# Three-part gathers and block-diagonal node products in a four-layer graph network on one core

## The chip, the cores and the metric

The kernel runs on one core of one Trainium2 chip. The metric is the device time of one execution in microseconds (us). A kernel's time is the median of its runs; one more execution is taken by the hardware profiler, and all rows come from that one.

## What is computed

The input has 6250 nodes with 64 features (`x`) and 200000 edges with a source, a destination, weights and attributes; the edges are sorted by destination. Four layers each compute `x = layernorm(x + layer(x))`:

```python
# layer 0: two spline convolutions (messages from two node products, mean by destination)
# layer 1: aggregation with attention over sources and over destinations
cat = jnp.concatenate((out, opinion, inn, inn_opinion), axis=1)
return cat @ weight + bias
# layer 2: three GCN convolutions, widths 16, 32 and 64
h = x @ w;  out = segment_sum(norm[:, None] * h[row], col);  return out + b
x2 = relu(gcn_conv(x, w1, b1, ...)); x3 = relu(gcn_conv(x2, w2, b2, ...)); x4 = relu(gcn_conv(x3, w3, b3, ...))
return jnp.concatenate([x, x4], axis=1) @ lw + lb
# layer 3: attention with a softmax over each destination's edges
score = leaky_relu(s_src + s_dst + s_edge, 0.2)
alpha = exp(score - max_per[dst]) / (denom[dst] + 1e-08)
out = segment_sum((z[src] + e) * alpha[:, None], dst);  return out + x
```

## The kernel before, in words

**Nodes.** A node array is held as 128 partitions x 49 node rows (`J` = 49) x features, in SBUF. A node product (`dense`, L83) multiplies every row by a small float32 weight matrix, 7 node rows (`GROUP_SLOTS`) at a time, so in 7 groups. For each group ScalarE copies the input rows to `xin` (L170), TensorE transposes them one node row at a time into PSUM (`turn`, L200, transposes L207), VectorE copies them to `xt` (`copy_out`, L125), TensorE multiplies node row by node row (`multiply`, matmuls L216), and VectorE adds the bias (L133) or ScalarE saves the result (L177). The buffers are double, and TensorE's order is turn(i+1), multiply(i). A float32 matmul call shows as two matmul rows in the trace (x14 for 7 calls). A product may have two inputs that add up (`K` = 2): then it has 14 transposes and 14 calls a group. With `prepare` the product runs beside fetches of its input: VectorE first makes the group's own part (L2204, L2205), ScalarE copies it, and there is one accumulator only.

The products that the change touches: layer 1's last, with the inputs `comb_src` (128 features) and `comb_lab` (16) and the weights `w_src` and `w_lab`; layer 2's `gw1` (64 to 16 features), `gw2` (16 to 32, beside fetches), `gw3` (32 to 64, beside fetches, behind a product with `lws[0]`) and the last, with `lws[1]` (64 to 64). The layer 1 product with `w_dst`, the one with `lws[0]`, and layers 0 and 3 keep their form.

**Edges.** The edges lie in 128 chunks, one per partition, of 1568 steps (`T`), and a pass goes through them 16 at a time (`B`), in 98 half-steps: a loop of 49 with the halves h = 0 and 1, whose buffers alternate. A half-step n fetches the table rows of its edges' sources. Some of the 16 are looked up on the chip: VectorE makes one-hot rows from keys (L938, `one_hots`), TensorE multiplies them with the table's parts (L920), VectorE picks out of the result (`pick`, L967) and sums (L970). The others are gathered by POOL with one indirect DMA each (`GATHERED` of them: 8 for tables of width 16, 10 for width 32, 12 in the softmax pass). Then VectorE weighs them (`msg`, L995 to L998) and runs a scan along the chunk (L1002). VectorE counts its instructions in the semaphore `stepped`; the marks FIRST_MADE, ONE_HOTS, SECOND_MADE, SCALED and MADE are counts within a half-step, after the first pick, the one-hots of the next half-step, the second pick, the weighing of the messages (SCALED, and in the softmax pass MADE). SP loads the keys, ScalarE stages the gather indices (L886) when the gathers of two half-steps before have landed, and stores go out on SP. POOL's loop in `graph_pass` (L866 to L882) is

```python
pool.wait_ge(indexed[h], i + 1)
pool.wait_ge(stepped, INIT + per * (2 * i + h - 2) + SCALED)
pool.sem_inc(sig["rounds"].sem, 1)
for k in range(GATHERED):
    pool.indirect_dma_start(out=rows[h][:, K + k, :], ...).then_inc(gathered[h], 16)
```

and the softmax pass has the same with MADE (L1484). `graph_pass` runs three times in layer 2 (width 16 twice, 9707 to 10740 and 10853 to 11880 us of the span, and width 32 once, 11982 to 13236.5), the softmax pass once in layer 3 (13486.5 to 15330). In the softmax pass VectorE picks at L1575, sums at L1578, makes one-hots at L1548, takes the gathers' scores at L1615, weighs at L1632 to L1637 and scans at L1642.

**Fetches.** After a pass, `complete_and_fetch` (L242) has POOL fetch 49 rows of results per partition (L269), 7 for each group of a product beside them.

**Setup.** At the start VectorE clears arrays, among them `w_labels` (L1914 on), then waits for `before_i`. SP loads 43 small weights (`later_weights`, L1755) during layer 0's last fetches. A block in layer 1 (L2055 to L2098) makes `w_lab` from the label weights with two matmuls, beside POOL's scatters (L1022). In layer 1 `class_keys` (L2167 to L2174) makes new keys on VectorE, with the dead front of `agg_dst` as scratch, and `turn_keys` stores them from SP (L799).

Of the kernel before, what the change touches and what calls it, by code (L numbers as in the profile page):

```python
# [17 lines left out]
F32 = mybir.dt.float32  # L18
# [64 lines left out]
def dense(nc, sig, xs, weights, out, width, store=None, bias=None, block=None, scope=None, prepare=None, ready=0):  # L83
# [7 lines left out]
    with ExitStack() as ctx:  # L91
# [3 lines left out]
        k_dims = [w.shape[0] for w in weights]  # L95
# [5 lines left out]
        xt = [sb(f"xt{k}_", [d, G, P]) for k, d in enumerate(k_dims)]  # L101
# [97 lines left out]
        def _(pe):  # L199
            def turn(i, b):  # L200
# [606 lines left out]
def graph_pass(nc, sig, table, width, edge, parts, running, final, zeros):  # L807
# [11 lines left out]
    with ExitStack() as ctx:  # L819
# [51 lines left out]
        def _(pool):  # L871
            with pool.Fori(0, IT) as i:
                for h in range(2):
# [5 lines left out]
                    for k in range(GATHERED):  # L879
                        pool.indirect_dma_start(out=rows[h][:, K + k, :], out_offset=None, in_=table,  # L880
# [505 lines left out]
def softmax_pass(nc, sig, table, edge, attrs, w_row, parts, running, final, zeros):  # L1386
# [14 lines left out]
    with ExitStack() as ctx:  # L1401
# [73 lines left out]
        def _(pool):  # L1475
            with pool.Fori(0, IT) as i:
                for h in range(2):
# [5 lines left out]
                    for k in range(GATHERED):  # L1483
                        pool.indirect_dma_start(out=rows[h][:, K + k, :], out_offset=None, in_=table,  # L1484
# [276 lines left out]
def gnn(nc, out, x, src, dst, u, ew, labels, label_rows, attrs, spline1, root1, bias01, spline2, root2, bias02,  # L1761
# [3 lines left out]
    with ExitStack() as ctx:  # L1765
# [39 lines left out]
        for name in ("ident", "ones", "upper", "shift1", "shift2"):  # L1805
# [21 lines left out]
        w_ef, w_lab, twt = sb("w_ef", [C, 2, C]), sb("w_lab", [2 * LABELS, C]), sb("twt", [C, 3 * LABELS])  # L1827
# [3 lines left out]
        w1, w2, w3 = sb("gw1s", [C, 16]), sb("gw2s", [16, 32]), sb("gw3s", [32, C])  # L1831
        gb = [sb(f"gb{k}", [P, c]) for k, c in enumerate((16, 32, C))]
        lws = [sb(f"lws{k}", [C, C]) for k in range(2)]
        lbs = sb("lbs", [P, C])
        wns, wnt, a_cols = sb("wns", [C, C + 2]), sb("wnt", [C, C]), sb("a_cols", [C, 2])
# [6 lines left out]
            (w1[:], gw1), (w2[:], gw2), (w3[:], gw3), (gb[0][:], gb1.broadcast_to([P, 16])), (gb[1][:], gb2.broadcast_to([P, 32])),  # L1842
# [520 lines left out]
```

## Time and profile before

| | |
|---|---|
| median of 3 runs | 15446.13 us (15444.47 to 15448.31) |
| the profiled execution's own time | 15444.99 us |
| its span in the profile | 15443.3 us |
| mean granted TensorE clock | 0.689 |
| TensorE (PE) busy | 7260.8 us, 47% of the span |
| VectorE (DVE) busy | 9169.8 us, 59% |
| ScalarE (ACT) busy | 2508.3 us, 16% |
| GpSimd (POOL) busy | 10805.1 us, 70% |

PE, DVE, ACT, POOL and SP are the engines; PEld is TensorE's weight load, SPq an engine's DMA issue. An engine is busy while it executes; waiting and issuing aren't counted. The kernel is a chain of stages, so a stage's limit is seen only in its own stretch. The granted clock is given in parts of 2.4 GHz: 0.50 is 1.2 GHz. Ends of matmuls are modelled, so that starts are the better measure. A matmul row's first numbers are the partitions and columns of the weight side, then the shape of what flows through.

### The profile page before, as it was taken

What the parts mean: (1) busy time and instruction counts of PE and PEld (TensorE: products, weight loads), DVE (VectorE), ACT (ScalarE), POOL (GpSimd) and SP (SyncE); (2) the same over time, 40 slices, a digit from 0 to 9 for tenths busy, and PEclk for the clock granted to TensorE, in tenths of its full rate; (3) what the DMA queues carried; (4) which work ended last, traced back from release to release, by engine and by line L of the source; (5) the groups of instructions that cost most, each with busy time, mean ns of one, the idle gap of its engine ahead of it and who ended that gap; (6) DMA issues with size and microseconds to landing.
All of it is one profiled execution on the core that took longest, in us unless ns stands there. A gap on an engine that the chain in (4) does not pass through costs nothing. (4 is left out here: it accounts for less than half of the span.)

```text
span 15443.3 us, 186434 instructions
## 1 busy us (share of the span) xinstructions
PE 7260.8 (47%) x53190; PEld 4887.6 (32%) x53190; DVE 9169.8 (59%) x21286; ACT 2508.3 (16%) x6533; POOL 10805.1 (70%) x10524
## 2 busy tenths in 40 slices
PE   3333333333320010001001355886787999699997
PEld 2222222222210000000000113786786555444443
DVE  5555554444444444444444796665665777587776
ACT  2222212222210000000000232111111111122222
POOL 6777777777767777777777301677777777588886
PEclk6555555555555555555555565998998999699998
DMA  2222223333323333333333574121211222122222
GB/s 81 70 71 72 71 64 95 103 103 101 103 83 94 94 99 94 93 99 94 93 97 96 202 272 149 39 44 37 43 43 36 48 49 50 26 72 72 71 73 60
DMA packets 631953, 1295.15 MB, mean 84 GB/s; under 512 B 219505, under 2 KB 366134, under 8 KB 606402
## 3 DMA queue, kind: packets, MB, share of 16 engines
q1 hardware_dynamic: 279776, 776.44, 14.4%
q0 software_dynamic: 337792, 456.35, 13.8%
q10 hardware_dynamic: 14337, 61.82, 1.1%
q8 instruction: 17, 0.28, 0.0%
q14 instruction: 31, 0.25, 0.0%
HBM read 623.75 MB, written 671.67 MB: 84 GB/s over the span
## 5 line engine op out<-in xcount | busy, mean ns | idle before, releaser
L521 POOL DMA_INDIRECT rows<-spline_table,index x3136 | 3181.4, 1014 | 1097.5 <-issue 973.9
L880 POOL DMA_INDIRECT rows<-gcn_table,index x2548 | 2515.9, 987 | 1008.1 <-issue 720.5
L920 PE MATMUL p_slots<-part,one_lo 128*128 128x208 bf16 (+1 forms) x25872 | 2973.8, 278 | 449.5 <-DVE one_lo L938 449.4
L920 PEld LDWEIGHTS p_slots<-part,one_lo 128*128 128x128 bf16 x25872 | 2372.6, 98 | 1050.2 <-DVE one_lo L938 492.9
L1116 POOL DMA_INDIRECT sent<-a_msg,a_place x1568 | 1625.9, 1037 | 478.0 <-issue 477.7
L1108 POOL DMA_INDIRECT a_rows<-att_table,a_index x1568 | 1486.2, 948 | 484.7 <-issue 477.2
L1170 PE MATMUL a_p_score<-tw_att,a_label 128*128 128x16 f32 x196 | 59.0, 381 | 3632.0 <-DMA a_label_row<-in_label_rows 3632.0
L1484 POOL DMA_INDIRECT e_rows<-soft_table,e_index x1176 | 1468.8, 1249 | 375.4 <-issue 328.8
L1526 PE MATMUL e_p_slots<-soft_part,e_one_lo 128*128 128x455 bf16 x8232 | 1644.7, 362 | 0.0
L1204 DVE TENSOR_TENSOR a_product<-a_rows,a_xdst 128x1024 f32<-128x1024 f32 x98 | 120.1, 1226 | 2067.2 <-DMA a_rows<-att_table,a_index 2067.2
L680 DVE TENSOR_TENSOR msg<-rows,weight 128x1024 f32<-128x1024 f32 x196 | 241.2, 1230 | 1814.2 <-DMA rows<-spline_table,index 1814.2
L1170 PEld LDWEIGHTS a_p_score<-tw_att,a_label 128*128 128x128 f32 x196 | 49.3, 311 | 3776.5 <-issue 3776.0
L1526 PEld LDWEIGHTS e_p_slots<-soft_part,e_one_lo 128*128 128x128 bf16 x8232 | 814.0, 99 | 798.2 <-issue 49.5
L617 PE MATMUL p_seen<-seen_hi,ident_b 128*128 128x49 bf16 x392 | 92.3, 235 | 2037.6 <-DVE seen_lo L692 2037.6
L688 DVE SCALAR_TENSOR_TENSOR run<-run,keep,msg 128x65 f32<-128x65 f32 (+1 forms) x3136 | 896.3, 286 | 111.9
L967 DVE TENSOR_TENSOR picked<-p_slots,one_hi 128x832 f32<-128x832 f32 (+1 forms) x588 | 684.5, 1164 | 308.0 <-PE p_slots L920 301.6
L617 PEld LDWEIGHTS p_seen<-seen_hi,ident_b 128*128 128x128 bf16 x392 | 50.1, 128 | 2080.6 <-DVE seen_lo L692 2080.6
L970 DVE TENSOR_REDUCE rows<-picked 128x64 f32<-128x832 f32 (+1 forms) x588 | 681.0, 1158 | 10.2
L547 ACT ACTIVATE earlier<-p_same 128x1280 bf16<-128x1280 f32 x392 | 484.9, 1237 | 680.1 <-PE p_same L609 678.8
L995 DVE TENSOR_TENSOR msg<-rows,weight 128x256 f32<-128x256 f32 (+1 forms) x294 | 217.4, 739 | 605.7 <-DMA rows<-gcn_table,index 602.0
L1380 DVE SCALAR_TENSOR_TENSOR s_run<-s_run,s_pen,s_msg 128x128 f32<-128x128 f32 x1568 | 541.4, 345 | 0.1
L1235 DVE SCALAR_TENSOR_TENSOR a_run<-a_run,a_pen,a_msg 128x128 f32<-128x128 f32 x1568 | 536.3, 342 | 0.0
(430 smaller groups left out, 14929.7 us busy)
## 6 DMA issues: line engine op xcount, KB each, us to landing
running_dst<-a_run SPq DMA_DIRECT2D x98, 1600.0 KB
running_src<-s_run SPq DMA_DIRECT2D x98, 1600.0 KB
running<-e_run_rows SPq DMA_DIRECT2D x98, 656.0 KB
s_rows<-sent ACTq DMA_DIRECT2D x98, 584.0 KB, 7.0
keys<-key_rows SPq DMA_DIRECT2D x200, 256.0 KB, 3.3
running<-run SPq DMA_DIRECT2D x98, 520.0 KB
rows<-spline_table,index POOLq DMA_INDIRECT x3136
running<-run SPq DMA_DIRECT2D x98, 512.0 KB
```

The costliest lines, as they stand in the source:

```text
L521: pool.indirect_dma_start(out=rows[h][:, k, :], out_offset=None, in_=table, in_offset=offsets(index[h][:, k:k + 1])).then_inc(gathered[h], 16)
L688: step(nc.vector.scalar_tensor_tensor(run[h][:, k, :], before, keep[h][:, k:k + 1], msg[h][:, k, :], ALU.mult, ALU.add))
L880: pool.indirect_dma_start(out=rows[h][:, K + k, :], out_offset=None, in_=table, in_offset=offsets(index[h][:, k:k + 1])).then_inc(gathered ...
L920: ins = nc.tensor.matmul(to, one_lo[h][:, q, e:e + P], flat(part[:, q, :, :]), start=q == 0 and part_no == 0, stop=q == CLASSES - 1 and pa ...
L967: step(nc.vector.tensor_tensor(picked[g][:], slots(g), mask, ALU.mult))
L970: step(nc.vector.tensor_reduce(rows[h][:, GROUPS[g], :], picked[g][:], AX.X, ALU.add))
L1108: pool.indirect_dma_start(out=rows[h][:, k, :], out_offset=None, in_=table, in_offset=offsets(index[h][:, k:k + 1])).then_inc(gathered[h], 16)
L1116: pool.indirect_dma_start(out=sent, out_offset=offsets(place[h][:, k:k + 1]), in_=msg[h][:, k, 0:SENT], in_offset=None).then_inc(scattered ...
L1235: step(nc.vector.scalar_tensor_tensor(run[h][:, k, SUMS:RUN], before[:, SUMS:RUN], pen[h][:, k:k + 1], msg[h][:, k, IN0:WIDE], ALU.add, AL ...
L1380: step(nc.vector.scalar_tensor_tensor(run[h][:, k, SUMS:RUN], before[:, SUMS:RUN], pen[h][:, k:k + 1], msg[h][:, k, LABELS:LABELS + 2 * C] ...
L1484: pool.indirect_dma_start(out=rows[h][:, K + k, :], out_offset=None, in_=table, in_offset=offsets(index[h][:, k:k + 1])).then_inc(gathered ...
L1526: ins = nc.tensor.matmul(p_slots[g][:, k, 0:Z * WIDE_CLASS], one_lo[h][:, q, e:e + P], flat(part[:, q, :, :]), start=q == 0 and part_no == ...
```

## The change

It has two parts. (1) POOL's gathers of a half-step n are divided: in `graph_pass` before gather GATHERED // 2 (4 or 5) stands a further wait, for ONE_HOTS of half-step n-1, with a semaphore increment; in the softmax pass there are two, before gather 4 for ONE_HOTS and before gather 8 for SECOND_MADE of half-step n-1. The first wait stays. (2) `dense` takes `pack`: s node rows are transposed at once (s x features up to 128 partitions), and multiplied at once with a weight that is block-diagonal, s times the width in columns. `gw1` and `lws[1]` are packed by 2 (4 transposes and 4 calls a group; the last pair overlaps the one before by a row), `gw3` by 4 (2 and 2), `gw2` by 7 (1 and 1). In layer 1's two-input product the label input is packed by 7: one call of 448 columns with start, then 7 calls with `w_src`. For this the weights are laid out with zeros between: 4 more memsets (L1918, 640 columns in all), 43 small loads become 54, and `w_lab` (112 x 448) is made by a wider product, 3 more VectorE operations and a multiply by a mask. `comb_lab` and the scratch of `class_keys` move to other parts of `agg_dst`, which makes their access strided.

```diff
@@ dense
-        k_dims = [w.shape[0] for w in weights]
+        pack = pack or [1] * K
+        k_dims = [w.shape[0] // s for w, s in zip(weights, pack)]
+        starts = [[min(o, G - s) for o in range(0, G, s)] for s in pack]
...
-        xt = [sb(f"xt{k}_", [d, G, P]) for k, d in enumerate(k_dims)]
+        xt = [sb(f"xt{k}_", [s * d, len(o), P]) for k, (d, s, o) in enumerate(zip(k_dims, pack, starts))]
...
-                    ins = nc.vector.tensor_copy(flat(xt[k][b][:]), flat(tp[k][0:k_dims[k], 0:G, :]))
+                    ins = nc.vector.tensor_copy(flat(xt[k][b][:]), flat(tp[k][0:pack[k] * k_dims[k], 0:len(starts[k]), :]))
...
-                    for g in range(G):
-                        ins = nc.tensor.transpose(tp[k][0:k_dims[k], g, :], xin[k][b][:, g, :], sig["ident"][:])
+                    for m, o in enumerate(starts[k]):
+                        ins = nc.tensor.transpose(tp[k][0:pack[k] * k_dims[k], m, :], flat(xin[k][b][:, o:o + pack[k], :]), sig["ident"][:])
...
-                for g in range(G):
-                    for k in range(K):
-                        ins = nc.tensor.matmul(acc[b % ACCS][:, g, 0:width], xt[k][b][:, g, :], weights[k], start=(k == 0), stop=(k == K - 1))
+                to = acc[b % ACCS]
+                if K == 2 and pack[1] == G:
+                    nc.tensor.matmul(to[:, 0:G, 0:width], xt[1][b][:, 0, :], weights[1], start=True, stop=False)
+                    for g in range(G):
+                        ins = nc.tensor.matmul(to[:, g, 0:width], xt[0][b][:, g, :], weights[0], start=False, stop=g + 1 == G)
+                else:
+                    for m, o in enumerate(starts[0]):
+                        for k in range(K):
+                            ins = nc.tensor.matmul(to[:, o:o + pack[k], 0:width], xt[k][b][:, m, :], weights[k], start=(k == 0), stop=(k == K - 1))
@@ graph_pass, POOL
                     for k in range(GATHERED):
+                        if k == GATHERED // 2:
+                            pool.wait_ge(stepped, INIT + per * (2 * i + h - 1) + ONE_HOTS)
+                            pool.sem_inc(sig["rounds"].sem, 1)
                         pool.indirect_dma_start(...)
@@ softmax_pass, POOL
                     for k in range(GATHERED):
+                        if k == GATHERED // 3:
+                            pool.wait_ge(stepped, INIT + per * (2 * i + h - 1) + ONE_HOTS)
+                            pool.sem_inc(sig["rounds"].sem, 1)
+                        if k == 2 * GATHERED // 3:
+                            pool.wait_ge(stepped, INIT + per * (2 * i + h - 1) + SECOND_MADE)
+                            pool.sem_inc(sig["rounds"].sem, 1)
                         pool.indirect_dma_start(...)
@@ weights and setup
+            *((w1_two[k * C:(k + 1) * C, k, :], gw1) for k in range(2)), *((w2_all[k * 16:(k + 1) * 16, k, :], gw2) for k in range(GROUP_SLOTS)),
+            *((w3_four[k * 32:(k + 1) * 32, k, :], gw3) for k in range(4)),
...
+            *((lws1_two[k * C:(k + 1) * C, k, :], lw[C:2 * C, :]) for k in range(2)),
...
-                    step(V.memset(w_labels[:], 0.0))
+                    for t in (w_labels, w1_two, w2_all, w3_four, lws1_two):
+                        step(V.memset(t[:], 0.0))
@@ label block
+                        for k in range(2):
+                            step(V.tensor_copy(label_sides[k][:], repeat(twt[:, k * LABELS:(k + 2) * LABELS], GROUP_SLOTS)))
+                        step(V.tensor_reduce(w_lab_at[:], sig["ident"][0:LABEL_ROWS, 0:LABEL_ROWS].rearrange("p (k l) -> p k l", l=2 * LABELS), AX.X, ALU.add))
...
-                        step(V.tensor_copy(w_lab[:], ps[0:2 * LABELS, C:2 * C]))
+                        step(V.tensor_tensor(w_lab[:], repeat(ps[0:LABEL_ROWS, C:2 * C], GROUP_SLOTS), spread(w_lab_at[:], C), ALU.mult))
@@ layer 1
-                    in_class = flat(agg_dst[:])[:, 0:T]
+                    in_class, key, low, high = agg_dst[:, :, 2 * C:2 * C + T // J], by_row(src_key), by_row(src_lo), by_row(src_hi)
...
-            dense(nc, sig, [comb_src, comb_lab], [w_src[:], w_lab[:]], y, C, bias=y)
+            dense(nc, sig, [comb_src, comb_lab], [w_src[:], flat(w_lab[:])], y, C, bias=y, pack=(1, GROUP_SLOTS))
@@ layer 2
-                dense(nc, sig, [agg[2]], [w3[:]], x4, C, bias=gb[2][:], block=block, scope=scope, prepare=own_part)
+                dense(nc, sig, [agg[2]], [flat(w3_four[:])], x4, C, pack=(4,), bias=gb[2][:], block=block, scope=scope, prepare=own_part)
-            dense(nc, sig, [xs], [w1[:]], x2, 16)
+            dense(nc, sig, [xs], [flat(w1_two[:])], x2, 16, pack=(2,))
-            ... dense(nc, sig, [agg[1]], [w2[:]], x3, 32, bias=gb[1][:], block=block, scope=scope, prepare=own_part)
+            ... dense(nc, sig, [agg[1]], [flat(w2_all[:])], x3, 32, pack=(GROUP_SLOTS,), bias=gb[1][:], block=block, scope=scope, prepare=own_part)
-            dense(nc, sig, [x4], [lws[1][:]], y, C, bias=y)
+            dense(nc, sig, [x4], [flat(lws1_two[:])], y, C, bias=y, pack=(2,))
```

## Rows read from the trace of the kernel before

**Rows 1.** Stretches: from:to, length, busy us (x instructions) of each engine, TensorE clock, DMA share, GB/s

```profile
9564.10:9642.10 78.00, 73.74 (x294) 59.47 (x294) 18.91 (x21) 7.84 (x14) 0.00 (x0) 0.57 0.00 0
9661.60:9697.10 35.50, 33.07 (x147) 28.78 (x147) 7.58 (x7) 5.54 (x14) 0.00 (x0) 0.50 0.00 0
...
13331.30:13367.60 36.30, 33.54 (x147) 28.73 (x147) 11.94 (x14) 3.92 (x7) 0.00 (x0) 0.50 0.00 1
...
11982.00:13236.50 1254.50, 1242.55 (x7056) 690.86 (x7056) 957.99 (x1186) 203.39 (x594) 941.73 (x980) 1.00 0.23 49
13486.50:15330.00 1843.50, 1670.93 (x8428) 832.02 (x8428) 1443.46 (x2856) 503.72 (x841) 1468.83 (x1176) 0.97 0.28 71
```

**Rows 2.** Waits, softmax pass, 13600 to 15200: us in total, times, longest

```profile
POOL e_rows L1484 <- issue: 286.7, 941, 0.3
DVE e_score L1615 <- DMA e_rows<-soft_table,e_index: 237.5, 86, 3.4
```

**Rows 3.** Waits, width-16 pass, 9800 to 10700

```profile
DVE msg L995 <- DMA rows<-gcn_table,index: 273.6, 85, 4.5
```

**Rows 4.** Timeline, width-16 pass: start, us, instruction, idle before and releaser

```profile
9858.73 0.94 POOL L880 DMA_INDIRECT rows<-gcn_table,index  x1 [2.01 <-issue]
...
10198.41 1.73 DVE L938 TENSOR_SCALAR one_lo<-keys,lanes 128x1024 bf16<-128x1024 f16 x4
...
10205.18 0.94 POOL L880 DMA_INDIRECT rows<-gcn_table,index  x1 [0.30 <-issue]
...
10210.39 1.36 POOL L880 DMA_INDIRECT rows<-gcn_table,index  x1 [0.30 <-issue]
```

**Rows 5.** Timeline, softmax pass

```profile
14098.95 1.11 DVE L1575 TENSOR_TENSOR e_picked<-e_p_slots,e_one_hi 128x910 f32<-128x910 f32 x1
...
14103.24 0.94 POOL L1484 DMA_INDIRECT e_rows<-soft_table,e_index  x1 [0.30 <-issue]
...
14109.39 3.38 POOL L1484 DMA_INDIRECT e_rows<-soft_table,e_index  x1 [0.30 <-DVE e_msg L1637]
...
14116.82 0.94 POOL L1484 DMA_INDIRECT e_rows<-soft_table,e_index  x1 [0.30 <-issue]
```

**Rows 6.** Timeline, width-32 pass

```profile
12402.73 1.41 DVE L938 TENSOR_SCALAR one_lo<-keys,lanes 128x768 bf16<-128x768 f16 x4
...
12408.00 0.94 POOL L880 DMA_INDIRECT rows<-gcn_table,index  x1 [0.30 <-issue]
```

**Rows 7.** Timeline, the two-input product, PE

```profile
9570.89 3.22 PE L207 MATMUL tp<-ident,xin 128*128 128x128 f32 x14 [2.26 <-DVE xt L125]
```

**Rows 8.** Timeline, a one-input product, PE, beside gathers

```profile
9488.18 1.70 PE L207 MATMUL tp<-ident,xin 128*128 128x128 f32 x7
...
9489.67 3.09 PE L216 MATMUL acc<-w_dst,xt 128*128 128x64 f32 x14
```

**Rows 9.** Timeline, two matmul calls of 512 columns, PE

```profile
8702.53 3.78 PE L1342 MATMUL s_p_ef<-w_labels,s_label_t 128*128 128x512 f32 x4 [0.37 <-ACT s_label_t L1305]
```

**Rows 10.** Timeline, gw3's product beside the last fetches

```profile
13306.11 0.94 POOL L269 DMA_INDIRECT gagg<-running,end_dst  x1 [0.30 <-issue]
...
13327.91 0.62 DVE L133 TENSOR_TENSOR x<-acc,gb 128x448 f32<-128x448 f32 x1 [3.40 <-PE acc L216]
```

**Rows 11.** Timeline, gw2's product behind the last fetches

```profile
11951.00 0.94 POOL L269 DMA_INDIRECT gagg<-running,end_dst  x1 [0.30 <-issue]
...
11954.55 1.65 PE L207 MATMUL tp<-ident,xin 128*16 128x128 f32 x7 [3.89 <-ACT xin L170]
...
11963.09 0.39 DVE L133 TENSOR_TENSOR x<-acc,gb 128x224 f32<-128x224 f32 x1 [3.34 <-PE acc L216]
```

**Rows 12.** Timeline, setup, the weights' loads, the class keys beside fetches

```profile
10.05 0.98 DVE L1924 CAST dst_f<-dst_i 128x1568 f32<-128x1568 int32 x1 [4.13 <-DMA before_i<-in_dst]
...
4446.49 0.41 SPq L799 DMA_DIRECT2D wide_key_rows<-turned_keys  x1
...
9539.37 0.39 SPq L799 DMA_DIRECT2D key_rows<-turned_keys  x1
```

More of the change, by code:

```diff
@@ L80, in offsets, with dense @@
     return bass.IndirectOffsetOnAxis(ap=ap, axis=0)
-def dense(nc, sig, xs, weights, out, width, store=None, bias=None, block=None, scope=None, prepare=None, ready=0):
+def dense(nc, sig, xs, weights, out, width, store=None, bias=None, block=None, scope=None, prepare=None, ready=0, pack=None):
     G = GROUP_SLOTS
@@ L1830, in gnn @@
         att_b, mix = sb("att_b", [P, C]), sb("mix", [P, 3])
-        w1, w2, w3 = sb("gw1s", [C, 16]), sb("gw2s", [16, 32]), sb("gw3s", [32, C])
         gb = [sb(f"gb{k}", [P, c]) for k, c in enumerate((16, 32, C))]
-        lws = [sb(f"lws{k}", [C, C]) for k in range(2)]
+        lws = [sb("lws0", [C, C])]
         lbs = sb("lbs", [P, C])
+        w1_two, w2_all, w3_four, lws1_two = sb("w1_two", [2 * C, 2, 16]), sb("w2_all", [GROUP_SLOTS * 16, GROUP_SLOTS, 32]), sb("w3_four", [P, 4, C]), sb("lws1_two", [2 * C, 2, C])
         wns, wnt, a_cols = sb("wns", [C, C + 2]), sb("wnt", [C, C]), sb("a_cols", [C, 2])
@@ L1841, in gnn @@
             *((w_labels[k * LABELS:(k + 1) * LABELS, k, :], trans) for k in range(B)),
-            (w1[:], gw1), (w2[:], gw2), (w3[:], gw3), (gb[0][:], gb1.broadcast_to([P, 16])), (gb[1][:], gb2.broadcast_to([P, 32])),
-            (gb[2][:], gb3.broadcast_to([P, C])), (lws[0][:], lw[0:C, :]), (lws[1][:], lw[C:2 * C, :]), (lbs[:], lb.broadcast_to([P, C])),
+            *((w1_two[k * C:(k + 1) * C, k, :], gw1) for k in range(2)), *((w2_all[k * 16:(k + 1) * 16, k, :], gw2) for k in range(GROUP_SLOTS)),
+            *((w3_four[k * 32:(k + 1) * 32, k, :], gw3) for k in range(4)), (gb[0][:], gb1.broadcast_to([P, 16])), (gb[1][:], gb2.broadcast_to([P, 32])),
+            (gb[2][:], gb3.broadcast_to([P, C])), (lws[0][:], lw[0:C, :]), *((lws1_two[k * C:(k + 1) * C, k, :], lw[C:2 * C, :]) for k in range(2)), (lbs[:], lb.broadcast_to([P, C])),
             (wns[:, 0:C], wn), (wnt[:], wn_t), (wes[:], we), (wet[:], we_t), (ae[:], att_edge), (a_cols[:, 0:1], att_src), (a_cols[:, 1:2], att_dst)]
@@ L2039, in gnn @@
                 t1 = sb("t1", [P, J, 2 * C + 1], F32, rows)
+                label_sides = [sb(f"label_side{k}", [C, GROUP_SLOTS, 2 * LABELS], F32, rows) for k in range(2)]
+                w_lab_at = sb("w_lab_at", [GROUP_SLOTS * 2 * LABELS, GROUP_SLOTS], F32, rows)
                 with ExitStack() as c2:
@@ L2156, in gnn @@
                 fetched.base += 16
-            comb_dst, comb_lab = sb("comb_dst", [P, J, 2 * C], F32, tmp), sb("comb_lab", [P, J, 2 * LABELS], F32, tmp)
+            comb_dst = sb("comb_dst", [P, J, 2 * C], F32, tmp)
+            comb_lab = agg_dst[:, :, RUN - 2 * LABELS:RUN]
             with ExitStack() as rows:
@@ L2167, in class_keys, with by_row @@
                 def class_keys(step):
[L2169 to L2170 removed]
+                    def by_row(t):
+                        return t[:, 0:T].rearrange("p (j c) -> p j c", j=J)
+                    in_class, key, low, high = agg_dst[:, :, 2 * C:2 * C + T // J], by_row(src_key), by_row(src_lo), by_row(src_hi)
+                    step(V.tensor_copy(key, low))
                     for q in range(CLASSES - 1, 0, -1):
[L2172 to L2174 removed]
+                        step(V.tensor_scalar(in_class, high, q * CLASS - 0.5, None, ALU.is_gt))
+                        step(V.scalar_tensor_tensor(key, in_class, float(P * q), key, ALU.mult, ALU.add))
+                        step(V.scalar_tensor_tensor(high, in_class, -float(CLASS * q), high, ALU.mult, ALU.add))
                 complete_and_fetch(nc, sig, (link_s, step_pen_s, use_pen_s), final, SUMS, RUN, fix_src, running_src, end_src, agg_src,
```

15 lines of the change are left out of this document (6 added, 9 removed).

## The prediction

> **What bounds the kernel now.** I read the page's slices first. They show a kernel of stages, and only four stages of its second half are touched, so an average over the span says little. I then cut out the touched stretches [rows 1]. Three are node products with TensorE busy for 73.74 of 78.0 us, 33.07 of 35.5 and 33.54 of 36.3, and nothing else near it: there every matmul counts. The width-32 pass has PE busy for 1242.55 of 1254.5 us at clock 1.00: PE bounds it, POOL (941.73) doesn't. The softmax pass has POOL and PE both under the stretch (1468.83 and 1670.93 of 1843.5), so its waits had to be read: POOL pauses only for its own issue, 0.30 us 941 times, while VectorE waits for the gathers 86 times, 237.5 us in all [rows 2]. POOL sets the pace there, and likewise in the two width-16 passes, where VectorE's `msg` waits 273.6 us for gathers [rows 3]. The timelines show a width-16 gather each 1.25 us (0.95 and a gap of 0.30), some stretched to 1.36 [rows 4], and in the softmax pass one of 3.38 beside VectorE's scan [rows 5].
>
> **The gathers' waits: 0.** The change adds one wait per half-step (49 x 2) in each graph pass, two in the softmax pass: 98 in each of three passes and 196 in the fourth. The first wait of a half-step stays, so by the waits alone no gather starts earlier; they can cost, or move gathers beside other work. Are they met when POOL comes to them? Width 16: gather 4 of a half-step starts at 10210.39 (the half-step's first is 10205.18); it would wait for the one-hots of the half-step before, done at 10198.41+1.73 = 10200.14, 10 us earlier [rows 4]. Softmax: gather 4 starts at 14109.39 and gather 8 at 14116.82 (the first is 14103.24); the later condition, the second pick, ended at 14100.06 [rows 5]. Width 32: gather 5 starts at 12408.00, the one-hots ended at 12404.14 [rows 6]. So all are met, by 9 to 17, 10 and 3.9 us. Behind POOL's wait only its own gathers are queued, and VectorE and ScalarE wait for those. A met wait's own price shows at a half-step's first gather, where POOL already passes two waits and a semaphore increment: the gap is 0.30 as at any other [rows 4, 5]. I take 0; the bounds are 0 and a second gap of 0.30 for each.
>
> **The two-input product (layer 1): -30.6.** Seven groups of 14 transposes and 14 matmul calls become 8 transposes, 7 calls with `w_src` and one call of 448 columns. Prices at the same clock: seven transposes start to start take 9489.67-9488.18 = 1.49, or 0.213 each; seven single calls 3.09 [rows 8]; a call of 512 columns 3.78/2 = 1.89 with its modelled end [rows 9], so some 1.5 for 448 (the last 0.2 to 0.4 us being end; I take 1.72 per 512, an estimate). A group takes 8x0.213+3.09+1.50 = 6.29, seven 44.0 against 73.74 [rows 1]: 29.7 less. VectorE's copy of the label block shrinks from 16x896 to 112x128, some 0.9 us of the 2.26 that PE waits once at the head [rows 7]. Lower bound of the gain: if the seven calls keep the 0.52 us that the 98 calls average now ((73.74-7x3.22)/98), 7x(3.64-3.09) = 3.9 less, and with the wide call at 1.89, 2.7 less again: 24; upper 34, if the calls reach the clock that this stretch has now in part (0.57 on average) all the time that it has it now.
>
> In gw1's stretch PE is busy for 93% of the time, yet its granted clock is 0.50, the 1.2 GHz level; in lws1's too, and 0.57 on average in the two-input product's [rows 1]. I price all by the lower level. The Trainium skill (TensorE: Matmul & The Clock Gate, What's actually happening) states that a TensorE that has been busy goes to 2.4 GHz; by it some 40 us more would go, and gw1's stretch does not agree with it.
>
> **gw1: -14.6, lws1: -14.8.** Seven transposes and seven calls per group become four and four; a call costs by its issue rather than by its columns (3.09 for seven of 64 columns [rows 8], and gw1's of 16 columns fill 33.07/7-1.49 = 3.23 for seven). 33.07x3/7 = 14.2 and 33.54x3/7 = 14.4 [rows 1], and 0.4 each for a copy of 128x512 instead of 64x896 at the head. Lower bound: if K = 128 instead of 64, or the wider result, adds a tenth to each call, 1.5 off each.
>
> **gw3, beside the last fetches: -12.9.** POOL's last fetch starts at 13306.11, the last bias at 13327.91 and ends at 13328.53 [rows 10]. The product lags now; with 2 transposes and 2 calls of 256 columns (0.86 each by the same 1.72 per 512) it keeps up with 7 fetches, 8.75 us a group. After the last fetch 3.55 us pass to the last turn, as with gw2 (11951.00 to 11954.55 [rows 11]), then turn 0.43, call pair 1.72, bias 0.62, pair 1.72, bias 0.62 and some 0.8 of handing over: 13315.6. Bounds 8 (the backlog behind the lws0 product isn't caught up) and 15.
>
> **gw2: -5.9.** From 11954.55 [rows 11] one transpose 0.21, call of 224 columns 0.75, bias 0.39, call 0.75, bias 0.39 and 0.5 of handing over: 11957.6, not 11963.48. Bounds 4 and 7.
>
> **Edits at nothing.** Four memsets at setup (640 columns) lie before VectorE's idle 4.13 us for `before_i` [rows 12]; without it 1 us. Eleven small weight loads on SP, past which no later issue is moved until its next, at 4446.49 [rows 12]; without cover, 0.5 each, 5.5. The label block (3 small VectorE operations, a wider product) lies beside POOL's scatters: 1 us if bare. The class keys' strided scratch comes before the key store at 9539.37, 25 us ahead of the product's stretch [rows 12, 1]; it could also hold up POOL's fetches. Together I allow -1 to +4.
>
> **The sum.** 30.6+14.6+14.8+12.9+5.9 = 78.8, bounds 62 to 86. The profiled execution took 15444.99 (span 15443.3), 1.1 under the median 15446.13. So 15366 for the profiled one and 15367 for the median.
>
> **Rivals.** *Each new wait costs POOL a gap.* In the width-16 and softmax passes POOL sets the pace, and 2x98+196 = 392 waits at 0.30 [rows 2, 4] are 118 us: 15446-79+118 = 15485, slower. It decides from 79/392 = 0.20 us a wait. Against it: the same 0.30 at the half-steps' first gathers. For it: the trace has no wait between two gathers of a batch.
>
> *The phase of the passes moves.* About every 14th half-step of the width-16 passes POOL pauses 2.01 instead of 0.30 [rows 4], in the other passes never, and neither wait nor transfer ends it. It may hang on how many instructions POOL runs; two or three more per half-step could double or remove it: seven times 1.71 us in a pass, 12 us, +-24 in two passes. And which gathers fall beside VectorE's work decides how many are stretched (1.36 for 0.94 [rows 4]): half of such a stretch more or less per half-step is 0.2x196, +-40 over two passes: 15327 or 15407.
>
> *The waits bind and move gathers away from VectorE's long operations.* A gather beside the scan takes 3.38 instead of 0.94 [rows 5]. If the split put such pauses where they cost nothing, the softmax pass would fall toward PE's 1670.93 [rows 1], 145 us at most with its edges: 15222. Against it: the conditions are met 9 us before. The Trainium skill (SBUF — State Buffer, SBUF: two separate sides) states that VectorE and GpSimd share one port pair under a lock held for a whole instruction; the 3.38 beside a scan agrees with it, and by it a gather moved out of the scan's time is a gain.
>
> *TensorE's clock rises in the products.* Fewer but longer calls may hold the 2.4 GHz level that the two-input product had in part [rows 1]: half of the 44+19+19 us that are left, 41 less, 15326. Against it: gw1 at 0.50 with PE busy for 93%.
>
> *The products gain half*, since copies between the engines bound them instead of PE: 15446-40 = 15406.
>
> **How the numbers follow.** Forecast 0.65, phases 0.10 (half either way), half gain 0.09, a gap per wait 0.09, gathers moved 0.04, clock 0.03. A measurement of this kernel tells some 0.2% (31 us) from no change. Faster than 15415: forecast, fast phase, moved gathers, clock, and three quarters of half gain and slow phase: 0.65+0.05+0.04+0.03+0.10 = 0.87. Slower than 15477: two thirds of the gap per wait, 0.06. Between: 0.07. The range leaves out the gap per wait and the moved gathers, 0.13, and the ends of the phases together with a bound: low 15325 (bound 86 and 35 of a fast phase), high 15425 (bound 62, the edits' 4 and a slow phase of 37).
>
> **What would show it.** PE's busy time in the two-input product near 44 us, gw1's and lws1's stretches some 14 us shorter each, the last gw3 bias near 10 us behind the last fetch; POOL's gaps before gathers 4 and 8 at 0.30, no wait for VectorE there, and the passes' stretches as long as now, 1254.5 and 1843.5 us [rows 1]. It is wrong if gaps of 0.6 stand there, or if the passes' lengths move by more than 20 us.

## The result and the profile after

The changed kernel took 15350.07 us (median of 4 runs, 15349.06 to 15352.87), the kernel before beside it 15447.22 (4 runs): a ratio of 0.9937, with a 95% interval of 0.992 to 0.9955. It is 97 us faster, where 79 were forecast; 15350 lies in the range of 15325 to 15425. The profiled execution took 15350.53 us (span 15348.8, granted clock 0.690), 94.5 less span than before.

The stretches of the changed kernel that answer to [rows 1], in the same order and with the same columns, then the two-input product's cut in two:

```profile
9567.10:9597.10 30.00, 27.64 (x168) 23.82 (x168) 13.39 (x21) 6.66 (x12) 0.00 (x0) 0.79 0.00 0
9617.20:9636.20 19.00, 17.70 (x84) 17.22 (x84) 4.84 (x7) 4.88 (x13) 0.00 (x0) 0.50 0.00 1
13252.30:13267.30 15.00, 13.17 (x84) 12.09 (x84) 8.97 (x14) 3.26 (x6) 0.00 (x0) 0.77 0.00 1
11914.00:13169.00 1255.00, 1243.06 (x7056) 690.73 (x7056) 961.14 (x1186) 203.63 (x594) 942.34 (x980) 1.00 0.24 49
13386.60:15232.20 1845.60, 1673.29 (x8428) 832.81 (x8428) 1443.88 (x2856) 503.87 (x841) 1470.90 (x1176) 0.97 0.29 71
9567.10:9578.40 11.30, 9.73 (x40) 8.55 (x41) 3.20 (x5) 3.25 (x6) 0.00 (x0) 0.50 0.00 0
9578.40:9597.10 18.70, 17.91 (x130) 15.26 (x128) 10.19 (x16) 3.41 (x6) 0.00 (x0) 0.97 0.00 0
```

The three products shrank from 78.0, 35.5 and 36.3 us to 30.0, 19.0 and 15.0. From first turn to last bias or save, by the timelines, they went from 76.7 to 29.8, 34.6 to 18.9 and 35.5 to 14.9. The two passes stayed: 1254.5 and 1255.0, 1843.5 and 1845.6. The width-16 passes, from their first gather to their last, took 1033.8 and 1035.1 us before and 1034.0 and 1032.4 now. What I had not counted on is the clock, the third column from the end: the granted clock went from 0.57 to 0.79 in the two-input product and from 0.50 to 0.77 in lws1's, and stayed at 0.50 in gw1's. The last two lines show when: 0.50 up to 9578.4, then 0.97, with PE busy for 17.91 of 18.7 us.

TensorE's timeline there, one group at the lower level and one at the upper:

```profile
9570.61 1.94 PE L209 MATMUL tp<-ident,xin 128*128 128x128 f32 x8 [1.47 <-DVE xt L127]
9572.35 1.70 PE L219 MATMUL acc<-w_lab,xt 112*128 112x448 f32 x2
9573.84 3.09 PE L221 MATMUL acc<-w_src,xt 128*128 128x64 f32 x14
9576.72 1.92 PE L209 MATMUL tp<-ident,xin 128*128 128x128 f32 x8
...
9584.40 1.04 PE L209 MATMUL tp<-ident,xin 128*128 128x128 f32 x8
9585.28 0.92 PE L219 MATMUL acc<-w_lab,xt 112*128 112x448 f32 x2
9586.03 1.67 PE L221 MATMUL acc<-w_src,xt 128*128 128x64 f32 x14
9587.54 1.04 PE L209 MATMUL tp<-ident,xin 128*128 128x128 f32 x8
```

The first group takes 9576.72-9570.61 = 6.11 us, 8 transposes, the call of 448 columns (9573.84-9572.35 = 1.49) and seven with `w_src`; my working had 6.29, with 1.50 for that call and 3.09 for the seven, where their starts give 9576.72-9573.84 = 2.88. The other group shown takes 9587.54-9584.40 = 3.14. Every term halves with the clock, the one whose price I took to be its issue too (2.88 to 9587.54-9586.03 = 1.51 for the seven). In lws1's product the calls go the same way (from the turn at 13259.30 on its rows are at the upper level):

```profile
13257.76 1.71 PE L225 MATMUL acc<-lws_two,xt 128*128 128x128 f32 x8
...
13259.74 1.06 PE L225 MATMUL acc<-lws_two,xt 128*128 128x128 f32 x8
```

The stretch of the two-input product before had been at the upper level for a part only: by its trace the clock rose three times, at about 9574.5, 9594.9 and 9615.5, right behind the transposes of every other group, and was back at 0.50 by 9578.2, 9598.7 and 9619.2, amid the short calls, though PE was busy throughout. At the upper level the calls of 16 and 128 rows in turn came each 0.36 us. Two cuts of it:

```profile
9574.50:9583.00 8.50, 8.50 (x40) 6.93 (x41) 2.44 (x3) 0.89 (x2) 0.00 (x0) 0.70 0.01 2
...
9604.00:9642.10 38.10, 37.41 (x139) 30.16 (x138) 8.62 (x10) 1.02 (x2) 0.00 (x0) 0.54 0.00 0
```

Behind the last fetches, gw3's product and gw2's, as in [rows 10, 11]:

```profile
13239.07 0.94 POOL L278 DMA_INDIRECT gagg<-running,end_dst  x1 [0.31 <-issue]
...
13243.38 1.91 PE L225 MATMUL acc<-w_four,xt 128*128 128x256 f32 x4
...
13248.19 0.62 DVE L135 TENSOR_TENSOR x<-acc,gb 128x448 f32<-128x448 f32 x1 [2.23 <-PE acc L225]
```

```profile
11888.60 0.94 POOL L278 DMA_INDIRECT gagg<-running,end_dst  x1 [0.30 <-issue]
...
11895.08 0.39 DVE L135 TENSOR_TENSOR x<-acc,gb 128x224 f32<-128x224 f32 x1 [1.27 <-PE acc L225]
```

gw3's product now ends 13248.81-13239.07 = 9.7 us behind the last fetch's start, not 22.4, and gw2's 6.9, not 12.5: 12.7 and 5.6 less, where 12.9 and 5.9 were forecast.

And POOL in the softmax pass, gathers 0, 3, 4 and 8 of a half-step, as in [rows 5]:

```profile
14004.43 0.94 POOL L1505 DMA_INDIRECT e_rows<-soft_table,e_index  x1 [0.30 <-issue]
...
14008.17 2.39 POOL L1505 DMA_INDIRECT e_rows<-soft_table,e_index  x1 [0.30 <-issue]
14010.86 3.38 POOL L1505 DMA_INDIRECT e_rows<-soft_table,e_index  x1 [0.30 <-DVE e_msg L1658]
...
14018.30 0.94 POOL L1505 DMA_INDIRECT e_rows<-soft_table,e_index  x1 [0.30 <-issue]
```

Gathers 4 and 8 have the new waits ahead of them, and the gap of 0.30 as any other. The same two gathers of a half-step are stretched as before, 3 and 4: on average over the 98 half-steps 2.14 and 3.27 us before, 2.15 and 3.24 now.

### The profile page after: what moved, and what is told of

Same layout as the page of the kernel before. It is cut to its first block and busy times, and to the rows that moved or that the text cites. A ratio compares the mean times of both kernels' runs of the same rounds, so it can differ in the third digit from the quotient of the medians.

```text
span 15348.8 us, 186466 instructions
## 1 busy us (share of the span) xinstructions
PE 7143.0 (47%) x52707; PEld 4786.5 (31%) x52707; DVE 9157.0 (60%) x21293; ACT 2508.0 (16%) x6533; POOL 10810.0 (70%) x10524
## 3 DMA queue, kind: packets, MB, share of 16 engines
q1 hardware_dynamic: 280272, 776.50, 14.6%
## 5 line engine op out<-in xcount | busy, mean ns | idle before, releaser
L1505 POOL DMA_INDIRECT e_rows<-soft_table,e_index x1176 | 1470.9, 1251 | 375.8 <-issue 293.5
```

## The experiments

Theory A: the products are the whole gain, and the added waits, being met, cost and bring nothing. Theory B: each wait costs a gap, hidden in a larger gain. Theory C: the divided gathers bring part of it. The kernel before was run with each set: 15441.49 us beside the first four, 15429.21 beside the next four, 15434.11 beside the last three. So each kernel is compared with its own set's kernel before.

**The waits alone.**

```diff
 kernel before, graph_pass (softmax_pass: k == GATHERED // 3 for ONE_HOTS, 2 * GATHERED // 3 for SECOND_MADE)
+    if k == GATHERED // 2:
+        pool.wait_ge(stepped, INIT + per * (2 * i + h - 1) + ONE_HOTS)
+        pool.sem_inc(sig["rounds"].sem, 1)
```

> The kernel before with the three added kinds of wait and nothing else. Theory A (the waits are met when POOL comes to them, and a met wait costs nothing): within 5 us of the kernel before, the passes' lengths within 3 us each, gaps of 0.30 us before gathers 4, 5 and 8. Theory B (the waits cost a gap of 0.30 each, and the products gave more than their measured stretches show): 118 us slower. Theory C (the divided gathers are part of the gain): 20 to 40 us faster.

Measured: 15441.76 (11 runs) against 15441.49, ratio 1.0 (0.9991 to 1.0009). The interval excludes B's 118 us (a ratio of 1.0076) and C's 20 to 40 (0.9974 to 0.9987).

**The packed products alone.**

```diff
 changed kernel, graph_pass (the two waits of softmax_pass likewise)
-    if k == GATHERED // 2:
-        pool.wait_ge(stepped, INIT + per * (2 * i + h - 1) + ONE_HOTS)
-        pool.sem_inc(sig["rounds"].sem, 1)
```

> The changed kernel without the added waits. Theory A: the changed kernel's 15350 within 5 us. Theory B: 118 us faster than it, 15232. Theory C: 20 to 40 us slower than it, 15370 to 15390.

Measured: 15346.91, 94.6 less than before, ratio 0.9938 (0.9924 to 0.9951). The changed kernel had 0.9937. Again A; B's 118 us are excluded, and C's least, 20 us, lies at the edge of these two intervals, so against C the run with the waits alone decides.

**A met wait before every gather.**

```diff
 packed products alone, graph_pass (softmax_pass with MADE)
     for k in range(GATHERED):
+        if k:
+            pool.wait_ge(stepped, INIT + per * (2 * i + h - 2) + SCALED)
+            pool.sem_inc(sig["rounds"].sem, 1)
```

> The packed products, and before every gather but a half-step's first a wait for the count that the first one has already waited for, with a semaphore increment: 2x98x7 in the width-16 passes, 98x9 in the width-32 pass, 98x11 in the softmax pass, 3332 met waits, 2450 of them where POOL sets the pace. Theory A (a met wait costs POOL nothing beside the 0.30 us gap): 15347 within 5 us. Theory B, by a gap each: 735 us slower. Between them: 10 ns a wait are 25 us.

Measured: 15333.76 against 15429.21, 95.5 less, where the packed products alone had 94.6 less. That is the same to 1 us. But the two intervals together leave some 30 us open, so by the times alone the 2450 waits in the passes where POOL sets the pace cost at most some 13 ns each, far from a gap of 300. The groups of POOL's softmax gathers say the same more sharply. The columns are count, busy us and mean ns, then idle us before them and what ended it. In this order: the kernel before, the waits alone, the changed kernel, and a met wait before every gather:

```profile
L1484 POOL DMA_INDIRECT e_rows<-soft_table,e_index x1176 | 1468.8, 1249 | 375.4 <-issue 328.8 <-DVE e_msg L1637 29.3 <-DVE e_run L1555 17.4
```

```profile
L1496 POOL DMA_INDIRECT e_rows<-soft_table,e_index x1176 | 1468.3, 1249 | 375.3 <-issue 292.2 <-DVE e_msg L1649 29.3 <-DVE e_one_hi L1563 29.0
```

```profile
L1505 POOL DMA_INDIRECT e_rows<-soft_table,e_index x1176 | 1470.9, 1251 | 375.8 <-issue 293.5 <-DVE e_msg L1658 29.2 <-DVE e_one_hi L1572 28.0
```

```profile
L1499 POOL DMA_INDIRECT e_rows<-soft_table,e_index x1176 | 1466.1, 1247 | 375.6 <-issue 245.6 <-DVE e_msg L1652 29.3 <-DVE e_one_lo L1563 26.8
```

The idle time is 375.3 to 375.8 us with 0, 2 or 11 waits more in each half-step. Only the attribution changes: more of the same gaps of 0.30 are put down to a VectorE instruction.

**A wait that isn't met.** This tests the rival by which a wait pays by keeping gathers out of VectorE's long operations.

```diff
 packed products alone, softmax_pass
+    if k == 3:
+        pool.wait_ge(stepped, INIT + per * (2 * i + h))
+        pool.sem_inc(sig["rounds"].sem, 1)
```

> The packed products, and in the softmax pass a wait before gather 3 for the end of the half-step before (its scan), which isn't met when POOL comes to it. Theory A (a wait that binds can only delay the gathers; VectorE's long operations cost POOL less than standing still): gathers 3 to 11 run behind the scan at 1.25 each, 11.25, and then 2.4 to land and 7.6 of VectorE's work: a half-step of 21 to 21.5 us instead of 18.65, 230 to 280 us slower. The rival that a wait pays by keeping gathers out of the scan's time: a half-step under 18.65, up to 145 us faster.

Measured: 15566.98 against 15429.21, ratio 1.0091 (1.0076 to 1.0106), 138 us slower than before and so 232 slower than the packed products (which were 94.6 faster than before); a half-step takes 21.0 us. POOL's group and its timeline at gather 3:

```profile
L1496 POOL DMA_INDIRECT e_rows<-soft_table,e_index x1176 | 1109.4, 943 | 968.2 <-DVE e_run L1654 611.3 <-issue 310.4 <-DVE e_run L1567 17.5
```

```profile
14112.54 0.94 POOL L1496 DMA_INDIRECT e_rows<-soft_table,e_index  x1 [0.30 <-issue]
14119.92 0.94 POOL L1496 DMA_INDIRECT e_rows<-soft_table,e_index  x1 [6.44 <-DVE e_run L1654]
```

Indeed no gather is stretched any more: 1109.4 us busy instead of 1468.8, the mean 943 ns. But POOL stands still for 593 us more. So of the 359 us that the stretched gathers cost, this wait wins all back on the gathers, and loses 593 by standing still while two gathers could have passed. A wait at another gather, or for a mark nearer to the scan's start, was not run.

**The two-input product alone.**

```diff
 packed products alone, layer 2
-    dense(nc, sig, [agg[2]], [flat(w3_four[:])], x4, C, pack=(4,), bias=gb[2][:], ...)
+    dense(nc, sig, [agg[2]], [w3_four[0:32, 0, :]], x4, C, bias=gb[2][:], ...)
-    dense(nc, sig, [xs], [flat(w1_two[:])], x2, 16, pack=(2,))
+    dense(nc, sig, [xs], [w1_two[0:C, 0, :]], x2, 16)
-    dense(nc, sig, [agg[1]], [flat(w2_all[:])], x3, 32, pack=(GROUP_SLOTS,), ...)
+    dense(nc, sig, [agg[1]], [w2_all[0:16, 0, :]], x3, 32, ...)
-    dense(nc, sig, [x4], [flat(lws1_two[:])], y, C, bias=y, pack=(2,))
+    dense(nc, sig, [x4], [lws1_two[0:C, 0, :]], y, C, bias=y)
```

> Only the two-input product of layer 1 is packed; gw1, gw2, gw3 and lws1 are as before, and no waits are added. The trace of the changed kernel gives this product some 48 us (from first turn to last bias about 76 down to 29), against my 30.6, since TensorE's clock rose to the 2.4 GHz level in it. If that is so and holds without the other edits: 15447-48 = 15399, and the clock at 1.00 from the third group on. If the rise comes from something that the other edits moved (the stretch's place in time), the product takes 45 us and the time is about 15416.

Measured: 15398.88 against 15441.49, 42.6 less, ratio 0.9973 (0.9963 to 0.9983). The product's stretch, and gw1's in its old form:

```profile
9561.20:9588.40 27.20, 24.99 (x168) 21.42 (x168) 13.39 (x21) 6.58 (x12) 0.00 (x0) 0.87 0.00 0
9608.60:9644.10 35.50, 33.06 (x147) 28.70 (x147) 8.12 (x8) 4.85 (x13) 0.00 (x0) 0.50 0.00 0
```

27.1 us from first turn to last bias, 49.6 less than before: the clock rises in this product without the other edits. The product's own time varies from trace to trace with the moment of the rise: packed, it took 26.9 to 29.8 us in the nine traces that have it in this form, and in its old form 76.7 in the kernel before and 74.3 in the one with the waits alone. The time shows 7 us less of gain than the stretch. Those 2.4 us are a part of it, 3.4 more stand behind the softmax pass, where the kernels with the new weights lose them (below; 1.6 come back ahead of this product), and the executions differ by as much again (the kernel before itself from 15435 to 15448).

**Seven label calls instead of one.** Is it the long call that raises the clock?

```diff
 packed products alone, multiply
-    nc.tensor.matmul(to[:, 0:G, 0:width], xt[1][b][:, 0, :], weights[1], start=True, stop=False)
     for g in range(G):
-        ins = nc.tensor.matmul(to[:, g, 0:width], xt[0][b][:, g, :], weights[0], start=False, stop=g + 1 == G)
+        nc.tensor.matmul(to[:, g, 0:width], xt[1][b][:, 0, :], weights[1][:, g * width:(g + 1) * width], start=True, stop=False)
+        ins = nc.tensor.matmul(to[:, g, 0:width], xt[0][b][:, g, :], weights[0], start=False, stop=True)
```

> As the packed products alone, but the label input, still transposed in one, is multiplied in seven calls of 64 columns (K = 112) instead of one call of 448. If the one long call is what raised the clock: the clock stays at 0.50 for most of the stretch and the two-input product takes 7 x (8 x 0.213 + 14 x 0.44) = 55 us. If fewer transposes do it, or any such stretch rises: about 14 x 0.22 + 8 x 0.13 = 4.1 us a group, 33 us in all with the head.

Measured: 15355.45 (one run). The stretch, and calls of it before and after the clock's rise:

```profile
9562.70:9602.00 39.30, 37.55 (x252) 37.06 (x252) 12.92 (x21) 6.64 (x12) 0.00 (x0) 0.73 0.00 0
```

```profile
9580.51 0.64 PE L220 MATMUL acc<-w_lab,xt 112*128 112x64 f32 x2
9580.94 0.63 PE L221 MATMUL acc<-w_src,xt 128*128 128x64 f32 x2
...
9584.42 0.39 PE L220 MATMUL acc<-w_lab,xt 112*128 112x64 f32 x2
9584.64 0.39 PE L221 MATMUL acc<-w_src,xt 128*128 128x64 f32 x2
```

39.7 us, between the two expectations: two groups at the lower level, the rest at the upper. So the one long call isn't needed for the rise. At the lower level a call follows the other after 0.43 us, though the label input still alternates with `w_src` and adds to the same sum; in the kernel before it was 0.617 at the same level (7.40 us for the twelve calls from 9583.50 to 9590.90). Two of its rows:

```profile
9625.31 0.69 PE L216 MATMUL acc<-w_src,xt 128*128 128x64 f32 x2
9625.93 0.69 PE L216 MATMUL acc<-w_lab,xt 16*128 16x64 f32 x2
```

What differs is the label input's contraction, 112 rows here and 16 there, and which of the two comes first.

**The old calls in another order.** That difference was tried on the kernel before.

```diff
 kernel before, multiply
-    for g in range(G):
-        for k in range(K):
-            ins = nc.tensor.matmul(..., start=(k == 0), stop=(k == K - 1))
+    for k in reversed(range(K)):
+        for g in range(G):
+            ins = nc.tensor.matmul(..., start=True, stop=True)
```

> The kernel before, with the two-input product's 14 calls of a group in another order: the seven with the label input (K = 16) first, then the seven with w_src (K = 128), instead of one after the other in turn. Each call starts its own sum, so the label input's part is left out of the result; the calls, their sizes and their number are the same. If the 0.617 us that a call takes in the record, against 0.41 to 0.43 for calls of one height, comes from the change of height from call to call: 0.19 x 12 = 2.3 us less a group, 16 us in all, and more if the clock rises. If it comes from the two inputs' number or from the clock alone: no change.

Measured: 15414.77 (10 runs) against 15434.11, 19.3 less, ratio 0.9987 (0.9977 to 0.9996). The stretch and its first group's calls:

```profile
9564.00:9624.10 60.10, 56.82 (x294) 49.84 (x294) 18.91 (x21) 6.61 (x12) 0.00 (x0) 0.59 0.00 0
```

```profile
9572.67 3.25 PE L216 MATMUL acc<-w_lab,xt 16*128 16x64 f32 x14
9575.85 3.25 PE L216 MATMUL acc<-w_src,xt 128*128 128x64 f32 x14
```

The seven K = 16 calls take 9575.85-9572.67 = 3.18, 0.454 each, and the product 59.7 us instead of 76.7 (or 74.3, in the trace of the waits alone), at nearly the same clock (0.59, and 0.57 or 0.59). So of the 46.9 us that the changed product gains, some 15 to 17 are the price of calls of 16 and 128 rows in turn, which packing the label input removed. This kernel leaves the label input's part out of the result, since each call starts its own sum. That the sums as such don't make the 0.617 is seen in the kernel with seven label calls, where pairs add up at 0.43; a kernel with the calls in this order and the right sums was not run.

**gw1 padded.** Its product is the one where the clock stayed low.

```diff
 packed products alone
-    dense(nc, sig, [xs], [flat(w1_two[:])], x2, 16, pack=(2,))
+    dense(nc, sig, [xs], [flat(w_labels[:])[:, 0:2 * C]], x2, 16, pack=(2,), columns=C)
 multiply
-    ... matmul(to[:, o:o + pack[k], 0:width], ...)
+    ... matmul(to[:, o:o + pack[k], 0:columns or width], ...)
```

> The packed products, with gw1's block-diagonal weight padded with zeros from 16 to 64 columns a row (calls of 128 columns instead of 32; the other columns are written and not read), which needs a memset of 0.9 us and two small loads beside earlier fetches. If what TensorE streams decides over its clock, as lws1's stretch (calls of 128 columns, clock risen) and gw1's (32 columns, 0.50 all through) suggest: the clock rises within gw1's stretch, and it takes about 14 us instead of 19, like lws1's. If it doesn't: calls of 128 columns at 0.47, the same 19 us or 0.5 more.

Measured: 15328.83 against 15429.21 (one run, 100.4 less). The stretch:

```profile
9608.40:9624.60 16.20, 13.75 (x84) 12.56 (x84) 5.66 (x8) 4.85 (x13) 0.00 (x0) 0.76 0.00 1
```

The clock rises to 0.76 on average, and the product takes 15.0 us instead of 18.9, though each call streams four times the columns, most of them zeros. The two kernels below have the same padding and repeat it (14.9 and 14.7 us, clock 0.75 and 0.76), where the six traces with gw1 packed but not padded all have 18.9 at 0.50. Which property of the work the chip answers to is not settled by this. The longer calls go with the upper level in this product and in lws1's, but length alone is not it: the kernel with seven label calls rose with calls of 64 columns, and the product with `w_dst`, with calls of 64 columns too and PE busy for 31.4 of 34.3 us, stays at 0.50 in every trace.

**More products packed.**

```diff
 gw1 padded, besides
-    dense(nc, sig, [xs], [wns[:]], t3, C + 2, nodes(soft_table), ...)
+    dense(nc, sig, [xs], [flat(w_labels[:])[:, WNS:WES]], t3, C + 2, nodes(soft_table), ..., pack=(2,))
-    dense(nc, sig, [attr_sum], [wes[:]], y, C, bias=y, ..., prepare=normalised)
+    dense(nc, sig, [attr_sum], [flat(w_labels[:])[0:GROUP_SLOTS * EDIM, WES:WNT]], y, C, bias=y, ..., prepare=normalised, pack=(GROUP_SLOTS,))
```

> The packed products without added waits, gw1 padded as in the run beside it, and two more products packed: layer 3's node product (64 to 66 features) by 2 and the one with the edge attributes' sums (16 to 64) by 7, its weights laid out later in a dead array. The node product: a ring of 4.82 becomes 2.7 at the low clock, 14 us over seven groups, up to 20 if the clock rises. The second product, behind the last fetches: from its last turn to its last bias 9.5 us now, 3.9 like gw2's with wider bias, 6 less. Padded gw1: 5. Together 15347-25 = 15322, 15317 to 15330.

Measured: 15329.59 against 15429.21, 99.6 less, only 5 better than the packed products and not 25. Layer 3's node product did fall from 36.4 to 17.9 us, by clock (0.50 to 0.79) and packing. But the next stage waits for POOL's scatters. The last save of the product and the fetch behind the scatters, in the packed kernel and in this one:

```profile
13322.48 0.56 ACT L179 ACTIVATE t<-acc 128x462 f32<-128x462 f32 x1 [3.40 <-PE acc L225]
...
13368.61 0.99 POOL L1035 DMA_INDIRECT first_rows<-soft_table,first_dst  x1 [0.30 <-issue]
```

```profile
13289.79 0.56 ACT L179 ACTIVATE t<-acc 128x462 f32<-128x462 f32 x1 [1.32 <-PE acc L225]
...
13352.51 0.99 POOL L1035 DMA_INDIRECT first_rows<-soft_table,first_dst  x1 [0.30 <-issue]
```

The product is done 46 us before that fetch in the one and 62 in the other: the gain became waiting. Besides, the late weight loads pushed the two-input product's first turn 3.5 us away from the product with `w_dst`.

**The loads earlier.**

```diff
 all packed
+    on_vector(nc, sig, lambda step: step(V.memset(flat(w_labels[:]), 0.0)), block)
+    moves(nc, sig, [...the loads...], block, after=sig["dve_step"].base)
     combine(agg_dst, 1, LABELS, 0, r_dst, comb_dst, block)
...
-    moves(nc, sig, [...the loads...], block, after=cleared)
```

> As the run with all products packed, but the memset of the dead array and the late loads stand at the start of the stage with the layer-1 fetches instead of behind its key store. There they ended about 3.5 us after the fetches and held up the two-input product. Expected 3.5 us less than that kernel, so 8 to 12 us faster than the changed kernel on the same chip: padded gw1 4, the product with the edge attributes' sums 6, layer 3's node product 1.6 (its 18 us lie beside POOL's scatters, which set that stage's end). If instead nothing hidden stands in the way: 25 us faster than the changed kernel.

> The changed kernel once more, beside the others on the same chip: 94 to 98 us faster than the kernel before.

Measured: 15326.23 with early loads and 15335.98 for the changed kernel, against 15434.11: 107.9 and 98.1 less. The two intervals, 0.9915 to 0.9942 and 0.9922 to 0.9949, overlap; the 9.8 us between them are as expected but not certain by the times alone. By the traces the two-input product starts 82.9 us behind the `w_dst` product's first turn, as in the changed kernel, and no longer 86.4. And the scatter behind the softmax pass is back at 0.99 us (below): the fetch behind it starts 25.3 us after the last gather, not 28.2 as with all packed.

## Why the prediction was right, and where its sizes were off

**The gathers' waits: 0.** Right, and now shown from three sides: alone (ratio 1.0), taken away (94.6 against 97.1 and 98.1 us), and multiplied (idle 375.6 us). Made to bind, a wait cost 232 us. The rival "each new wait costs POOL a gap" is dead: the pauses between two gathers of a batch behave as those at its first. So is "the waits move gathers away": gathers 3 and 4 are stretched as before.

**The two-input product: forecast 30.6, measured 46.9.** The group at the lower level was right to 0.2 us in 6.3. The mis-sized term is the clock: "I price all by the lower level". It was so for one group; the next took 4.53, and then each 3.14. I had the rise as a rival at 0.03, argued down by gw1's stretch, which of the three products that stand alone is the one where it did not come. The Trainium skill's statement (TensorE: Matmul & The Clock Gate, What's actually happening), that a busy TensorE goes to 2.4 GHz, agrees with this trace in the two-input product and in lws1's, and not in gw1's, busy for 17.70 of 19.0 us at 0.50. The untouched product with `w_dst` doesn't agree with it either (31.43 of 33.8 us, 0.50). I also took the seven calls' old price of 0.52 as a possible price of the new ones (the bound of 24). It was, for the most part, the price of calls of 16 and 128 rows in turn, as the reordered calls show (the average also mixes both levels), and it did not outlive the packing.

**lws1: forecast 14.8, measured 20.6**, by the same term: the clock rose at about 13259.2, 7 us into the product. **gw1: 14.6, measured 15.8**, at the clock I had assumed. **gw3: 12.9 and 12.7. gw2: 5.9 and 5.6.**

**The time is nearer than its parts.** The products together were forecast at 78.8, with bounds of 62 to 86, and gave 101.6: the rival of the clock, meant as 41 us more, came true for about half. Some 7 us were lost elsewhere, so that 97 came out. It is luck that the range held it: the products' own bound of 86 ends at 15446-86 = 15360, above 15350, and only the allowance for a fast phase of the passes, which did not come, carried the range down to 15325.

**Edits at nothing: allowed -1 to +4.** The five products give 101.6 us, the spans differ by 94.5. Two effects of the edits that I had not seen lie between, and both are on POOL beside VectorE. The first is a scatter behind the softmax pass, which starts 0.05 us after a long VectorE addition, in the kernel before and in the changed one (each time a row of VectorE's timeline, then the scatter as a group of one):

```profile
15338.33 3.50 DVE L2306 TENSOR_TENSOR twice<-xs 128x3136 f32<-128x3136 f32 x1 [0.23 <-DVE m_fixed L1710]
L1668 POOL DMA_INDIRECT running<-m_fixed,fix_dst x1 | 1.0, 986 | 4.8 <-DVE m_fixed L1710 4.8
```

```profile
15240.55 3.42 DVE L2340 TENSOR_TENSOR twice<-xs 128x3136 f32<-128x3136 f32 x1 [0.22 <-DVE m_fixed L1731]
L1689 POOL DMA_INDIRECT running<-m_fixed,fix_dst x1 | 4.2, 4226 | 4.7 <-DVE m_fixed L1731 4.7
```

It takes 4.23 us instead of 0.99, and the stretch from the last gather to the end 130.7 instead of 127.3. It is 4.22 or 4.23 in all nine traces that have the new weights and this order, and 0.98 or 0.99 in the three with the old ones. In the kernel with early loads VectorE starts 0.3 us after the scatter, and the scatter takes 0.99. What in the edits decides which of the two goes undisturbed is not shown.

The second effect is a gain: with the strided scratch, three of VectorE's operations for the class keys take 1.79 us instead of 0.97, so the keys are made 2.1 us later, yet POOL's 49 fetches beside them are busy for 58.6 us instead of 60.3, and the two-input product starts 82.9 us behind the first turn of the product with `w_dst` instead of 84.6.

The setup and the label block cost nothing: layer 0's first gather starts at 75.26 instead of 75.56, and from its last gather to layer 1's first it is 181.8 us in both. What remains is 3.2 us in layer 1's attention pass (4028.3 instead of 4025.1 from first to last gather), which no edit touches, 2.1 in the softmax pass (1825.9 to 1828.0), and some smaller ones. In the other kernels that don't hold POOL back the softmax pass takes 1821.9 to 1828.8, so I take these as the scatter of single executions (the changed kernel's second trace is from one of 15346.56, with a median of 15335.98).

**The phases of the passes: +-40 allowed.** They moved by 2.7 us at most in the width-16 passes, and the pause of 2 us still comes at every 14th half-step, six times in a pass, with one wait more in each half-step, and with seven more where a met wait stands before every gather. So it does not hang on the number of POOL's instructions; what ends it was not found.

**The products gain half, bounded by copies.** The two-input product was not: at the upper level PE is busy for 17.91 of 18.7 us.

## What to carry to other kernels

A wait that is met when its engine gets there cost nothing on POOL here; look up in the timeline when the awaited instruction ended and when the waiting engine arrives, and price the wait by that difference alone. Small float32 products with short contractions can gain by block-diagonal weights beyond the number of instructions: here calls of 16 rows in turn with calls of 128 had been slow, and the clock rose for most of the stretch in two products of three, so give such a change a second price at the upper level with a real chance. A stage that runs beside a longer one gives nothing, however much shorter it gets: find what the next stage waits for first. And an edit can change, far behind it, how long an indirect DMA of POOL takes beside a VectorE operation; compare the two traces stage by stage, not only the stages that were touched.

## What the runs showed of the hardware that I had not expected

- Calls of 64 columns with contractions of 16 and 128 rows in turn follow each other after 0.617 us at the lower clock; seven of 16 rows and then seven of 128 after 0.454 and 0.434 (each call with a sum of its own); calls of 112 and 128 rows in turn after 0.43.
- Widening gw1's calls from 32 to 128 columns with zeros made its stretch shorter, 15.0 for 18.9 us, since the granted clock went from 0.50 to 0.76 on average.
- 1078 met waits in the softmax pass, each with a semaphore increment, changed POOL's idle time before the gathers by 0.2 us (375.4 to 375.6).
- An indirect DMA of POOL that takes 0.99 us took 4.22 to 4.23 beside a VectorE addition of 3.42 us (128 x 3136 float32) in nine kernels, and 0.98 to 0.99 beside the same addition (then 3.50 us) in three.
